# Two cross-attention layers on one core: later weight blocks are split behind the gelu, and the last entry is finished on VectorE

## The reference

```python
# layer 0: attention of x over [context, x], 16 heads of 32
q  = x @ q_w + q_b
kv = concat([ctx, x], 1) @ kv_w + kv_b
a  = softmax(mask(q k^T / 32)) v
h  = rmsnorm(a @ out_w + out_b + x) * postnorm_w
y  = gelu_tanh(h @ mlp_w1 + mlp_b1) @ mlp_w2 + mlp_b2 + x      # 512 -> 2048 -> 512
# layer 1: grouped attention of y over ctx, 32 heads of 16 over 8 key heads
o  = softmax(q1 k1^T / 4 + add_mask) v1
z  = o @ Wo + bo + y
out = (z - mean(z)) * rsqrt(var(z) + 1e-6) * gamma + beta
```

## Time and profile before

| what | value |
|---|---|
| median of 3 runs | 1155.17 us (1154.1 to 1156.08) |
| profiled execution | 1155.72 us, span 1153.5 us |
| busy share of the span | PE 93%, PEld 79%, DVE 60%, ACT 56%, POOL 28% |
| mean granted TensorE clock | 0.978 |
| DMA | 71.16 MB, mean 62 GB/s |

### The profile page before, as it was taken

How to read it: one execution, slowest core, us unless ns; L and a number is a source line. 1 busy time by engine, 2 the same in 40 slices (tenths; PEclk the granted TensorE clock), 3 DMA queues, 4 the chain that set the end, 5 groups by cost and what they waited for, 6 DMA issues and landing times. The chain is left out here.

```text
span 1153.5 us, 27390 instructions
## 1 busy us (share of the span) xinstructions
PE 1078.4 (93%) x8976; PEld 912.7 (79%) x8976; DVE 690.8 (60%) x2683; ACT 648.5 (56%) x2204; POOL 321.7 (28%) x507
## 2 busy tenths in 40 slices
PE   5899999999999998599999999999978999999994
PEld 4788888888888886489899989998966877777772
DVE  4577777777777777562122112211337999999994
ACT  4545555555555555373333333333428999999993
POOL 1223333333333333200000000000001455555555
PEclk9999999999999999789999999999999999999997
DMA  8211111212111110275011010110211212221200
GB/s 287 76 40 49 50 49 57 63 53 65 48 48 48 48 46 10 82 236 158 1 55 54 2 55 19 35 55 1 74 37 59 70 52 67 77 77 50 66 22 28
DMA packets 65355, 71.16 MB, mean 62 GB/s; under 512 B 7056, under 2 KB 41104, under 8 KB 65296
## 3 DMA queue, kind: packets, MB, share of 16 engines
q1 hardware_dynamic: 65296, 70.42, 19.2%
HBM read 49.43 MB, written 20.97 MB: 61 GB/s over the span
## 5 line engine op out<-in xcount | busy, mean ns | idle before, releaser
L727 POOL TENSOR_TENSOR pr<-pr,rec 128x512 f32<-128x512 f32 x128 | 130.6, 1042 | 295.8 <-DVE rec L993 295.8
L1496 ACT ACTIVATE pr<-pr,nmax 128x128 f32<-128x128 f32 x512 | 198.2, 396 | 1.5 <-DVE nmax L1584 1.5
L1926 ACT ACTIVATE g_m<-J,b_part_m 128x256 f32<-128x256 f32 x128 | 60.7, 474 | 216.6 <-PE J L175 216.6
L832 ACT ACTIVATE pr<-pr,nmax 128x256 f32<-128x256 f32 x256 | 126.6, 501 | 3.5 <-DVE nmax L982 3.4
L1584 DVE CUSTOM_DVE_ANT_0 pr<-S,madd 128x128 f32<-128x128 f32 x512 | 114.0, 282 | 2.2 <-issue 1.2
L1903 POOL TENSOR_TENSOR resid_m<-resid_m,b_all_m 128x512 f32<-128x512 f32 x16 | 22.3, 1410 | 326.6 <-DMA resid_m<-in_x 326.6
L1496 ACT ACTIVATION_READ_ACCUMULATOR pr<-pr,nmax 128x1 f32 x512 | 100.2, 196 | 0.0
L982 DVE CUSTOM_DVE_ANT_0 pr<-S,madd 128x256 f32<-128x256 f32 x256 | 92.5, 418 | 8.3 <-PE S L1176 8.1
L175 PE MATMUL J<-nT0hi_m,uphi 128*128 128x256 f32 x256 | 73.0, 285 | 8.5 <-DVE uplo L163 5.1
L175 PE MATMUL J<-hThi,wkhi 128*128 128x256 f32 x256 | 74.8, 292 | 0.8 <-DVE wklo L157 0.8
L175 PE MATMUL J<-nT0hi_m,uplo 128*128 128x256 f32 x256 | 72.6, 284 | 0.0
(11 more groups left out here) (236 smaller groups left out, 3233.6 us busy)
## 6 DMA issues: line engine op xcount, KB each, us to landing
staged<-in_L_xattn_mlp_w SPq DMA_DIRECT2D x16, 512.0 KB, 4.4
rows<-in_ctx SPq DMA_DIRECT2D x16, 256.0 KB, 2.8
rows<-in_x SPq DMA_DIRECT2D x16, 256.0 KB, 3.0
kept_c<-hThi SPq DMA_DIRECT2D x16, 256.0 KB, 2.7
kept_c<-hTlo SPq DMA_DIRECT2D x16, 256.0 KB, 2.8
kept_n<-n_out SPq DMA_DIRECT2D x16, 256.0 KB, 2.4
n_in<-kept_n SPq DMA_DIRECT2D x16, 256.0 KB, 3.8
resid_m<-in_x SPq DMA_DIRECT2D x16, 256.0 KB, 2.9
```

The lines of the kernel that those rows point to most:

```text
L727: pool.tensor_tensor(part, part, by.unsqueeze(2).broadcast_to([P, per_bank, keys]), ALU.mult).then_inc(normed, 1)
L832: last = nc.scalar.activation(part, part, ACT.Exp, bias=nmax[slot][:, at], scale=-1.0, accum_out=den[slot][:, at])
L1496: last = nc.scalar.activation(pr[k][:, i, :], pr[k][:, i, :], ACT.Exp, bias=nmax[k][:, i:i + 1], scale=-1.0, accum_out=den[r][:, at:at + 1])
L1926: nc.scalar.activation(g[slot][:, :], J[j][:, 0:PR], ACT.Gelu_apprx_tanh, bias=b1_part[:, f, :]).then_inc(J_taken[j], 1)
```

## The change

It has two parts.

In the first pair of the middle stage the split of block f + 4 moves from the top of step f to behind the gelu and its two halves, on ScalarE and VectorE alike. On SyncE the wait for the stored entries moves from before the loads to just before the row loads.

In layer 1 the entry 15 no longer goes to GpSimd for its root, scale and shift. VectorE, right behind the guess, runs three Newton steps of two instructions, then (z - mean) * gamma and (that) * root + beta, and SyncE's store waits for a semaphore of its own (`last_ready`).

```diff
+    def last(self):
+        return self.it is None and self.n == B - 1
...
                 def store(e):
-                    sp.wait_ge(fin_ready, e.count(1, 1))
+                    if e.last():
+                        sp.wait_ge(last_ready, 1)
+                    else:
+                        sp.wait_ge(fin_ready, e.count(1, 1))
...
                 def root(e):
+                    if e.last():
+                        return
...
                 def affine(e):
+                    if e.last():
+                        return
...
+                    if e.last():
+                        finish_last(e)
+
+                def finish_last(e):
+                    y, t, h = (stat[:, c:c + 1] for c in (2, 3, 10))
+                    dve.wait_ge(guess_ready, e.count(1, 1))
+                    for step in range(NEWTON):
+                        nc.vector.scalar_tensor_tensor(t, y, h, y, ALU.mult, ALU.mult).then_inc(last_step, 1)
+                        dve.wait_ge(last_step, 2 * step + 1)
+                        nc.vector.scalar_tensor_tensor(y, t, 1.5, y, ALU.add, ALU.mult).then_inc(last_step, 1)
+                        dve.wait_ge(last_step, 2 * step + 2)
+                    dve.wait_ge(scaled, e.count(1, 1))
+                    dve.wait_ge(stored[e.s], e.uses(16))
+                    nc.vector.scalar_tensor_tensor(nrm[:, :], res[:, :], stat[:, 0:1], nw_all[:, :],
+                                                   ALU.subtract, ALU.mult).then_inc(last_step, 1)
+                    dve.wait_ge(last_step, 2 * NEWTON + 1)
+                    nc.vector.scalar_tensor_tensor(fin[e.s][:, :], nrm[:, :], y, nb_all[:, :],
+                                                   ALU.mult, ALU.add).then_inc(last_ready, 1)
...
                 def norm(e):
+                    if e.last():
+                        return
...
-                for s in range(2):
-                    sp.wait_ge(sems["n_stored"][s], 16 * (B // 2))
                 for u in range(staging.first[1], staging.first[2]):
                     if u not in staging.prefetched(1):
                         staging.load(sp, u)
                     if u == staging.prefetched(1)[-1] + 2:
+                        for s in range(2):
+                            sp.wait_ge(sems["n_stored"][s], 16 * (B // 2))
                         load_n(1)
...
                     for f in range(FC):
-                        if first and f + EARLY < 2 * (FC // 2):
-                            staging.take_hi(nc, act, u0 + f + EARLY, targets[u0 + f + EARLY])
                         j, n = w.use("J", 2)
...
                         nc.scalar.activation(gs[slot][0][:, :], g[slot][:, :], ACT.Copy).then_inc(g_hi, 1)
+                        if first and f + EARLY < 2 * (FC // 2):
+                            staging.take_hi(nc, act, u0 + f + EARLY, targets[u0 + f + EARLY])
```

More of the change, by code:

```diff
@@ L1343, in second_attention @@
         a_seen, rec_seen, moments_seen, scores_seen = map(sem, ("a_seen", "rec_seen", "moments_seen", "scores_seen"))
-        rec_wide = sem("rec_wide")
+        rec_wide, last_step, last_ready = map(sem, ("rec_wide", "last_step", "last_ready"))
         h_hi, q_hi, k_hi, exped = map(sem, ("h_hi", "q_hi", "k_hi", "exped"))
@@ L1952, in pair @@
                     for f in range(FC):
-                        if first and f + EARLY < 2 * (FC // 2):
-                            staging.take_lo(nc, dve, u0 + f + EARLY, targets[u0 + f + EARLY])
                         slot = f % RING
@@ L1958, in pair @@
                                                 ALU.subtract).then_inc(g_split, 1)
+                        if first and f + EARLY < 2 * (FC // 2):
+                            staging.take_lo(nc, dve, u0 + f + EARLY, targets[u0 + f + EARLY])
                         if not ahead and f in LATE:
```

## The result

The changed kernel takes **1148.0 us** (median of 12 runs, 1146.0 to 1151.94) against 1155.16 us (12 runs, 1152.41 to 1159.67): a ratio of 0.9937, 95% interval 0.9921 to 0.9954, so 7.2 us less (5.3 to 9.1). The forecast was 1146.0 in a range of 1144.0 to 1150.0. The time lies in the range; the gain is 2 us short of the 9.2 forecast. The profiled execution took 1148.85 us, span 1146.9, at a mean clock of 0.981. One later run of the changed kernel, 1530.78 us at a mean clock of 0.651, is left out of every figure here.

What follows compares the result with a forecast made beforehand. TensorE was taken to bound the middle stage and a chain of single instructions the run's end. Gap 3.1, clock 2.6 and end 3.6 sum to 9.3 us, giving 1146.0 us in a range of 1144.0 to 1150.0.

Steps and rivals of the forecast that it cites:

- The gap: Middle stage, first pair: the first gelu no longer waits for block 4, so TensorE resumes 3.11 us earlier.
- The drain that speaks against it: First gelu's table load: a skill's rule adds about 1.4 us of drain, making the gap's gain 1.7 us, not 3.1.
- The clock: Middle stage, resumption to second down product: without idle time the clock stays full, 2.59 us gained (bounds 0 and 2.6).
- Rival 1: Middle stage's first pair: the clock falls all the same, 2.6 us stay lost, 1148.5 us; chance 0.09.
- No new wait: Middle stage: later splits and block loads cause TensorE no new wait; taken as 0, bounds 0 and 5.7 us.
- the tightest place: Middle stage: gelu 3, behind block 6, frees its bank 1.1 us before TensorE's up product needs it.
- Rivals 2 and 4: Middle stage: 2, weight loads hold gelu 3 on, 1151.6 (0.07); 4, later splits slow the block ring, 1157.5 (0.03).
- The moved wait: Middle stage, SyncE: the wait for stored rows goes behind block 5's load; worth 0 either way.
- The end: Last entry's root, scale and shift on VectorE: store at 1147.44 in place of 1151.06, 3.6 us (bounds 3.2 and 3.7).
- rival 3: The end: the wide VectorE instruction waits for GpSimd, so the end gains nothing, 1149.5 us; chance 0.04.
- The sum of 9.2: Whole kernel: 3.1 + 2.6 + 3.6, given as 9.3 us in the prediction, for a forecast of 1146.0 us.

Runs made afterwards that it cites:

- the early table: Changed kernel plus a one-column gelu ahead of the first step, so the gelu table loads before the first product's end: 1147.61 us, ratio 0.9933.
- the fillers: Changed kernel plus unread TensorE work: 18 transposes before the middle stage, 13 products behind it, 8 before layer 1's query: 1143.82 us; last two only: 1146.24 us.
- the order alone: Kernel before with only the later blocks' splits moved behind the gelu on ScalarE and VectorE: 1151.25 us, ratio 0.9968.
- TensorE kept busy: Kernel before plus 27 unread products on TensorE between the second and third up product of the first pair: 1151.67 us, ratio 0.9965.
- the second set: Changed kernel run again, unaltered, beside later variants on one chip: 1146.95 us (6 runs), ratio 0.9931.

## Why the prediction was right, and where 2 us stayed

**The gap, 3.11 us: right.** From the first up product to TensorE's resumption it took 4.81 us where it was 7.87, 3.06 less; the idle time fell by 3.00 (3.40 to 0.40). Load to gelu took 1.30 against the 1.29 counted, and gelu to TensorE's resumption 0.53 as counted. From the first product's end (488.16 + 0.41 = 488.57) to the load it was 0.08 and not 0.04. That the wait lands on the table load was also right: the 1.74 us ahead of the load are released by PE, so its 1.28 us lie on the path, and loading it early gave 0.55 back.

**The drain that speaks against it: not there.** With the early table the load starts 0.01 us behind the split before it (484.92 + 1.04 = 485.96, load 485.97), and its first user comes 1.30 behind the load's start. The Trainium skill, "ScalarE: Activation LUTs", section "What ACT_TABLE_LOAD costs", adds a drain of about 1.4 us. Neither this trace nor that of after has it, and 3.11 was the better figure than 1.7.

**The clock, 2.59 us: right.** From resumption to the second down product it took 494.80 - 490.48 = 4.32 us, 4.22 forecast, 6.81 before: 2.49 gained, with the clock at 1.00 from 490 us on. Rival 1 (the clock falls all the same) is out. The reason given against it was weaker than it looked, though. From 440 to 460 us the kernel before kept clock 1.00 at 16.40 us of work, but the changed kernel's second trace has 0.83 there at 15.10 us.

**No new wait: right, but the tightest place was another.** Gelu 3 came at 497.41 and its bank, 0.53 behind it, 1.1 us before TensorE wanted it at 499.02, as reckoned. Gelu 1, behind block 4, came at 492.04; TensorE wanted its bank at 493.39 (0.70 behind the 492.69 at which the first down product's second half starts), 0.8 later. With the first products at full rate this slack is gone, as the fillers showed. Rivals 2 and 4 are out: TensorE waited for no block in after.

**The moved wait, 0: right** (1.0005). **The end, 3.6 us: right**, 3.66 from guess to store; rival 3 is out.

**The sum of 9.2 against 7.2 measured.** No step was mis-sized by more than 0.2 us: the terms hold where they were made. What the sum takes for granted is that the rest of the span costs the same, and in the profiled executions it does not. The profiled execution of after shows where. Its timeline of PE at the start of layer 1:

```profile
852.13 0.76 PE L175 MATMUL J<-uphi,hThi 128*128 128x512 f32 x1 [1.67 <-DVE hTlo L1551]
852.69 0.63 PE L175 MATMUL J<-uplo,hThi 128*128 128x512 f32 x1
...
856.96 0.59 PE L175 MATMUL J<-uphi,hTlo 128*128 128x512 f32 x1
...
866.40 0.39 PE L1753 MATMUL S<-KT0hi,QT0hi 32*128 32x256 f32 x4 [1.36 <-DVE KT0lo L1580]
```

and that of the order alone, with the same middle stage:

```profile
849.42 0.47 PE L175 MATMUL J<-uphi,hThi 128*128 128x512 f32 x1 [1.67 <-DVE hTlo L1541]
850.19 0.40 PE L175 MATMUL J<-uphi,hThi 128*128 128x512 f32 x1
...
859.92 0.39 PE L1723 MATMUL S<-KT0hi,QT0hi 32*128 32x256 f32 x4 [1.36 <-DVE KT0lo L1570]
```

The waits are the same to the hundredth; the query products take 0.63 in the one and 0.40 in the other, the low level of the clock and the high one. From query to scores TensorE idles 4.48 us in after, in before and in order only alike; it is busy 9.79, 7.45 and 6.02 us, at mean clocks of 0.70, 0.87 and 1.00. So this stretch differs in TensorE's rate alone, with the same work and the same waits. Without filler ahead of it, the stretch took 14.2 to 14.3 us in three executions with both parts of the change, 13.5 and 12.9 in two more, 13.9 with TensorE kept busy, 11.9 to 12.0 in before and the two kernels with its slow first pair, 10.5 in order only. Whether the earlier end of the middle stage makes the low clock likelier there or these are chance draws, one or two traced executions of each kernel can't tell. Nor is it sure that 2 us are missing over many runs: the interval of the ratio reaches 9.1 us, and the second set gave 8.0. So in the traces the shortfall is seen at that place, and its cause stays open.

## What to carry to other kernels

An in-order engine should not hold a wait for a transfer ahead of the instruction that frees the engine that sets the time: put the take behind it, and read off which bank or block is next, and by how much. Idle time of TensorE can cost twice, as here: 3.1 us itself and 2.5 in the clock that fell with it; both could be read from a row before the change was made. Cut two traces at common events and compare the pieces: that showed within 0.2 us what times with intervals of 2 to 3 us to either side could not.

## What was not expected of the hardware

- **Four bytes cost 3.1 us.** Buffers moved by 4 bytes on each partition make the up product 1.44 us on average and not 1.41, at clock 1.00 and without an idle gap that the trace shows (two kernels, 355.93 against 352.82 us in all the others).
- **The spread between runs goes with the clock.** Over 64 runs of before, 1151.04 to 1163.75 us, time and mean granted clock go together with a correlation of -0.94 and -0.8 us per 0.001 of clock. The same pieces of code took from 10.5 to 14.3 us (layer 1's start) and from 482.7 to 488.2 us (the whole first stage), and filler on TensorE at the stages' starts lowered the median from 1146.95 to 1143.82 us. What makes the clock differ between executions was not tried.
- **The clock falls in a pause, behind it, or not at all.** With TensorE kept busy it fell about 0.5 us into the work behind 1.78 us of idle time, in before within a pause of 3.40, and at the start of layer 1 in order only it stayed at 1.00 behind pauses of 1.81 and 1.67 us.
